# A graph and mixture-of-experts kernel on one NeuronCore: a fourth buffer for gathered rows, and inverse roots made on VectorE alone

## The reference

```python
x = x + gnn0(layernorm(x))   # h = n @ wl; sum over 100000 edges of w * h[src] into row dst; + n @ wr + biases
x = x + ffn0(layernorm(x))   # 8 experts on every node, mixed by gates
x = x + gnn1(layernorm(x))   # the same edges again, other weights
x = x + ffn1(layernorm(x))   # 32 experts, one chosen for each node

def ffn0(n):
    gate = softmax(n @ Wr + br)                       # [nodes, 8]
    h = relu(bn(n @ W1[e] + b1[e]))                   # for each expert e
    h = relu(bn(h @ W2[e] + b2[e]))
    return sum over e of gate[e] * (h @ Wo[e] + bo[e])

layernorm(x) = (x - mean) / sqrt(var + 1e-5)
bn(h) = g * (h - m) * rsqrt(v + 1e-3) + b
```

## Time and profile before

| | us |
|---|---|
| median of 3 runs | 2962.04 |
| lowest and highest | 2961.93, 2962.98 |
| the profiled execution, its own time | 2958.48 |
| its span (first to last instruction) | 2956.5 |

### The profile page before, as it was taken

How to read it: one execution, slowest core, us unless ns; L and a number is a source line. 1 busy time by engine, 2 the same in 40 slices (tenths; PEclk the granted TensorE clock), 3 DMA queues, 4 the chain that set the end, 5 groups by cost and what they waited for, 6 DMA issues and landing times. The chain is left out here.

```text
span 2956.5 us, 54481 instructions
## 1 busy us (share of the span) xinstructions
PE 2599.4 (88%) x19092; PEld 2420.7 (82%) x19092; DVE 2167.4 (73%) x5110; ACT 1565.7 (53%) x3295; POOL 1957.5 (66%) x1696
## 2 busy tenths in 40 slices
PE   5799935799999999999999994599999999999999
PEld 5799825788888888888888873489999999999999
DVE  8898836577787777777878754767777777777773
ACT  4477636788888888888888762111212112121212
POOL 0355557777777877777777501877777777777770
PEclk9999956799999999999999997689999999999999
DMA  2133454332333333233233203788888888888880
GB/s 74 6 82 77 93 137 144 91 97 78 109 108 91 99 108 110 79 107 110 78 115 108 80 1 114 212 205 214 204 215 214 212 208 215 213 213 209 212 212 24
DMA packets 241962, 390.31 MB, mean 132 GB/s; under 512 B 43642, under 2 KB 115218, under 8 KB 241426
## 3 DMA queue, kind: packets, MB, share of 16 engines
q0 software_dynamic: 163072, 310.24, 41.1%
q1 hardware_dynamic: 78324, 74.90, 8.0%
q10 hardware_dynamic: 288, 1.61, 0.1%
HBM read 343.43 MB, written 43.19 MB: 131 GB/s over the span
## 5 line engine op out<-in xcount | busy, mean ns | idle before, releaser
L1409 POOL DMA_INDIRECT f_got<-h_tab,list_cols x784 | 981.1, 1251 | 291.0 <-issue 219.1
L2121 POOL DMA_INDIRECT n_got<-h_tab,edge_cols x784 | 806.5, 1029 | 238.5 <-issue 227.6
L1690 DVE TENSOR_TENSOR f_hlo<-edge_cols,f_hhi 128x1024 fp32r<-128x1024 f32 (+1 forms) x208 | 242.0, 1163 | 294.3 <-ACT f_hhi L1498 294.1
L1585 PE MATMUL bank<-f_mhi,f_hot 128*128 128x256 f32 x1168 | 329.0, 311 | 131.2 <-DVE f_mlo L1684 131.1
L1468 ACT ACTIVATE f_got<-f_got,list_cols 128x256 f32<-128x256 f32 x784 | 333.9, 497 | 145.6 <-DMA f_got<-h_tab,list_cols 145.1
L2185 ACT ACTIVATE n_hrh<-bank 128x512 fp32r<-128x512 f32 x196 | 116.9, 597 | 535.6 <-PE bank L2254 535.6
L1585 PEld LDWEIGHTS bank<-f_mhi,f_hot 128*128 128x128 f32 x1168 | 247.6, 212 | 148.0 <-issue 143.8
L1493 ACT ACTIVATE edge_cols<-bank,f_shf,f_scl 128x512 f32<-128x512 f32 (+1 forms) x416 | 295.1, 743 | 106.9 <-PE bank L1400 76.7
L2232 PE MATMUL bank<-n_got,n_hot_h 128*128 128x256 f32 x784 | 242.2, 309 | 99.4 <-DMA n_got<-h_tab,edge_cols 59.0
L1586 PE MATMUL bank<-f_mlo,f_hot 128*128 128x256 f32 x1168 | 320.3, 304 | 0.0
L400 POOL DMA_INDIRECT list<-runs,off_i x98 | 158.0, 1612 | 215.2 <-DVE off_i L759 99.0
(11 more groups left out here) (331 smaller groups left out, 7833.0 us busy)
## 6 DMA issues: line engine op xcount, KB each, us to landing
f_got<-h_tab,list_cols POOLq DMA_INDIRECT x784
n_got<-h_tab,edge_cols POOLq DMA_INDIRECT x784, 3.8
n_rows<-acc_tab SPq DMA_DIRECT2D x24, 256.0 KB, 4.7
out_rows<-n_rows SPq DMA_DIRECT2D x24, 256.0 KB, 3.7
h_tab<-acc SPq DMA_DIRECT2D x37, 128.0 KB, 3.5
edge_cols<-in_w SPq DMA_DIRECT2D x16, 256.0 KB, 2.8
acc<-in_x SPq DMA_DIRECT2D x4, 896.0 KB, 7.9
h_tab<-hbuf SPq DMA_DIRECT2D x7, 512.0 KB
```

Of the source, the lines that this page charges most:

```text
L1409: nc.gpsimd.indirect_dma_start(got[:, s % RING0, u, :], None, h_tab[0], bass.IndirectOffsetOnAxis(gidx0[:, s * U + u:s * U + u + 1], 0), b ...
L1585: nc.tensor.matmul(tile_bank(t), lhs, mhi[:, s % 2, u, :], start=begins, stop=False)
L1690: nc.vector.tensor_tensor(hlo[l][:, :, 0:w], rl[:, :, 0:w], hhi[l][:, :, 0:w].bitcast(F32), ALU.subtract).then_inc(s_lo[l], 1)
L2121: nc.gpsimd.indirect_dma_start(got[:, s % RING, u, :], None, h_tab[1], bass.IndirectOffsetOnAxis(gidx[:, s * U + u:s * U + u + 1], 0), bou ...
```

## The change

Three edits, all in the second stage.

1. `RING0` is 4 instead of 3: four buffers for gathered rows, each for one slot (4 x 256 floats per partition). The tensor `x4` is gone; the third raw weight buffer now lies in the upper columns of `xraw`, which are not otherwise in use while weights load.
2. The square roots of both layer norms are no longer taken by ScalarE. VectorE computes the inverse root from `var` alone: it shifts the number's bits right by one, subtracts from a constant (the guess), and makes three Newton steps of three instructions each, 11 instructions (`ROOT_STEPS`) instead of 5. The waits for ScalarE (`s_sd`, `s_sd4`) are gone; VectorE waits for its own `s_var`, `s_var4`.
3. The root of batch norm is made by the same function, and its Sqrt on ScalarE is gone.

```diff
-RING0 = 3
+RING0 = 4
+SEED = float(0x5f3759df)
+ROOT_STEPS = 11
...
-            x4 = sb3("x4", [P, F, 2 * P])
...
-            raw = [rl[:, :, 0:D], rl[:, :, D:2 * D], x4[:, :, :]]
+            raw = [rl[:, :, 0:D], rl[:, :, D:2 * D], xraw[:, :, D:2 * D]]
...
-                    if s - 1 in READY:
-                        g = READY.index(s - 1)
-                        t, w = tile(g, 0), width(g)
-                        act.wait_ge(s_var, t + w)
-                        nc.scalar.activation(scale[:, t:t + w], var[:, t:t + w], ACT.Sqrt).then_inc(s_sd, 1)
...
-                    if s - 1 in DONE:
...
-                        nc.scalar.activation(scale[:, t:t + w], var[:, t:t + w], ACT.Sqrt).then_inc(s_sd4, 1)
...
-                        nc.scalar.activation(scl[:, :, :, :], bnt[:, :, :, :], ACT.Sqrt).then_inc(s_bnroot, 1)
...
+                def inverse_root(r, v, x, counter, base):
+
+                    bits, seed = v.bitcast(I32), r.bitcast(I32)
+                    nc.vector.tensor_scalar(x.bitcast(I32), bits, 1, None, ALU.arith_shift_right).then_inc(counter, 1)
+                    dve.wait_ge(counter, base + 1)
+                    nc.vector.tensor_scalar(seed, x.bitcast(I32), -1.0, SEED, ALU.mult, ALU.add).then_inc(counter, 1)
+                    for i in range(3):
+                        dve.wait_ge(counter, base + 3 * i + 2)
+                        nc.vector.tensor_tensor(x, r, r, ALU.mult).then_inc(counter, 1)
+                        dve.wait_ge(counter, base + 3 * i + 3)
+                        nc.vector.scalar_tensor_tensor(x, x, -0.5, v, ALU.mult, ALU.mult).then_inc(counter, 1)
+                        dve.wait_ge(counter, base + 3 * i + 4)
+                        nc.vector.scalar_tensor_tensor(r, x, 1.5, r, ALU.add, ALU.mult).then_inc(counter, 1)
+                    dve.wait_ge(counter, base + ROOT_STEPS)
...
                 def newton(t, w, counter, base):
-                    r, v, x = scale[:, t:t + w], var[:, t:t + w], nwt[:, t:t + w]
-                    nc.vector.reciprocal(r, r).then_inc(counter, 1)
...
-                    nc.vector.tensor_tensor(r, r, x, ALU.mult).then_inc(counter, 1)
-                    dve.wait_ge(counter, base + 5)
+                    inverse_root(scale[:, t:t + w], var[:, t:t + w], nwt[:, t:t + w], counter, base)
```

More of the change, by code:

```diff
@@ L1223, in build @@
             s_var = sem("f_var")
-            s_sd = sem("f_sd")
             s_newton = sem("f_newton")
@@ L1241, in build @@
             s_var4 = sem("f_var4")
-            s_sd4 = sem("f_sd4")
             s_newton4 = sem("f_newton4")
@@ L1483, in relus @@
                     if n == 0 and l == 0:
-                        act.wait_ge(s_bn, 10)
+                        act.wait_ge(s_bn, 5)
                         act.wait_ge(s_wlo, NPIECE)
@@ L1563, in _ @@
                             nc.scalar.activation(bos[at:at + EXPERTS0, :], braw, ACT.Copy).then_inc(s_bos, 1)
-                        act.wait_ge(s_bn, 1)
-                        nc.scalar.activation(scl[:, :, :, :], bnt[:, :, :, :], ACT.Sqrt).then_inc(s_bnroot, 1)
                     for i in range(s * PACE, min(s * PACE + PACE, NPIECE)):
@@ L1708, in add_out @@
                                                        ALU.mult, ALU.add).then_inc(s_out, 1)
-                def newton(t, w, counter, base):
-                    r, v, x = scale[:, t:t + w], var[:, t:t + w], nwt[:, t:t + w]
-                    nc.vector.reciprocal(r, r).then_inc(counter, 1)
[L1713 to L1719, removed]
-                    nc.vector.tensor_tensor(r, r, x, ALU.mult).then_inc(counter, 1)
-                    dve.wait_ge(counter, base + 5)
+                def inverse_root(r, v, x, counter, base):
[11 more added lines that the diff above has]
+                    dve.wait_ge(counter, base + ROOT_STEPS)
+                def newton(t, w, counter, base):
+                    inverse_root(scale[:, t:t + w], var[:, t:t + w], nwt[:, t:t + w], counter, base)
                 def logits(i):
@@ L1817, in _ @@
                         t, w = tile(g, 0), width(g)
-                        dve.wait_ge(s_sd, g + 1)
-                        newton(t, w, s_newton, 5 * g)
+                        dve.wait_ge(s_var, t + w)
+                        newton(t, w, s_newton, ROOT_STEPS * g)
                         if g:
@@ L1849, in _ @@
                         t, w = tile(g, 0), width(g)
-                        dve.wait_ge(s_sd4, g + 1)
-                        newton(t, w, s_newton4, 5 * g)
+                        dve.wait_ge(s_var4, g + 1)
+                        newton(t, w, s_newton4, ROOT_STEPS * g)
                         if g:
@@ L1873, in _ @@
                                                 bos[HI_A:HI_A + EXPERTS0, :].bitcast(F32), ALU.subtract).then_inc(s_bos, 1)
[L1874 to L1884, removed]
+                        dve.wait_ge(s_bn, 1)
+                        inverse_root(*(a[:, :, :, :].rearrange("p l e f -> p (l e f)") for a in (scl, bnt, shf)), s_bnroot, 0)
                         nc.vector.tensor_tensor(scl[:, :, :, :], scl[:, :, :, :], bnp[:, :, 1], ALU.mult).then_inc(s_bn, 1)
                         nc.vector.tensor_tensor(shf[:, :, :, :], bnp[:, :, 0], bnp[:, :, 3], ALU.subtract).then_inc(s_bn, 1)
-                        dve.wait_ge(s_bn, 8)
+                        dve.wait_ge(s_bn, 3)
                         nc.vector.tensor_tensor(shf[:, :, :, :], shf[:, :, :, :], scl[:, :, :, :], ALU.mult).then_inc(s_bn, 1)
-                        dve.wait_ge(s_bn, 9)
+                        dve.wait_ge(s_bn, 4)
                         nc.vector.tensor_tensor(shf[:, :, :, :], shf[:, :, :, :], bnp[:, :, 2], ALU.add).then_inc(s_bn, 1)
```

3 lines of the change are left out of this document (removed).

## The result

| | before | after |
|---|---|---|
| median, us | 2961.98 (4 runs) | 2933.11 (4 runs) |
| profiled execution, us | 2958.48 | 2933.08 |
| ratio to before, 95% interval | | 0.9893 (0.9876 to 0.991) |
| first gather of the second stage to first gather of the third, us | 1430.5 | 1404.5 |

The change makes the kernel 28.9 us faster by the medians and 25.4 by the profiled executions, where -33 was predicted. The last line of the table is 1837.3 - 406.8 against 1813.1 - 408.6: -26.0 us, all of the difference, in the second stage.

What follows compares the result with a forecast made beforehand. It took GpSimd's gathers to be as full as TensorE and their late edge stream to idle TensorE. -44 (ring) + 6 (gathers) + 0 (roots) + 4 (returning waits) + 1 (stage end) = -33 us: 2962 to 2929 us, range 2912 to 2952.

Steps and rivals of the forecast that it cites:

- GpSimd is as full as TensorE, and late gathers reach TensorE: Second stage, 609 to 1690 us: gathers fill 1017 of 1081 us; a 3.3 us GpSimd stall is paid back by TensorE.
- So every wait of the present pattern goes: Gathers waiting for a free buffer, 609 to 1690 us: four buffers allow 23.5 us for a 19.7 us lag, gain 44.
- my first rival: Second stage: the consumers are the limit, so the gain is 24 us, to 2938 us; chance 0.20.
- the second rival: Ring of gathers: a deeper ring only shifts the wait, leaving 44 us nearly whole, 2957 us; chance 0.06.
- Gathers lengthened by VectorE, +6: Gathers beside VectorE: same VectorE work in 3.5% less time, so a gather meets it 3.5% more often, +6 us.
- Roots 0 net: Layer norm roots: ScalarE's relief and VectorE's longer root taken as 0 us together, bounds -15 and +27.
- A root 2.54 us: Layer norm root on VectorE: nine two-input instructions at 0.20 and two `tensor_scalar`s at 0.37, 2.54 us instead of 1.18.
- The rival in which small `tensor_scalar`s wait out gathers: Roots on VectorE: two each wait for a whole gather, 26 us more, half on the path, 2942 us; chance 0.04.
- The end of the stage, +1: Last root, alone on the path to the second stage's end: 2.2 us instead of 1.29, +1 us.
- Slower, the longer roots pace VectorE: Rival: TensorE waits for `mlo` by all of each longer root, 27 us and 1, nothing from the ring, 2990 us; chance 0.05.
- The marks that I set: Profile after: `mlo` waits under 10 us, gathers 1.27 to 1.29, one Exp table load, group 102, last gather near 1640.

Runs made afterwards that it cites:

- e7: The changed kernel with `mlo` made ahead of the lower halves of the finished rows in slot 0 of a group: 2925.4 us, 0.986 of before.
- e8: As e7, and in one slot of each group `mlo` also made ahead of the output sums, only while there are edges: 2911.8 us, 0.981 of before.
- e9: The changed kernel with three buffers instead of four and one Newton step instead of three, roots still on VectorE: 2951.8 us, 0.995 of before.

## Why the prediction was right, and where its steps were not

**The time and its sign** were right: -28.9 us by the medians, -26.0 in the stage, for a forecast of -33, and inside the range. That the number came so near was in part luck, since large terms were wrong and made up for one another. As an account of GpSimd's time (where the time went, not what caused it):

| us | forecast | measured |
|---|---|---|
| waits for a full ring, all gathers (44.9 to 32.2) | -44 + 4 | -12.7 |
| length of the 784 gathers (981.1 to 959.2) | +6 | -21.9 |
| other pauses up to the last gather | 0 | -4.3 |
| from the last gather to the third stage | +1 | +13.0 |
| sum | -33 | -26 |

Of the steps:

- *GpSimd is as full as TensorE, and late gathers reach TensorE.* Right. The wait in front of `xhi` and its 2.36 us in place 11 were made by gathers: with four buffers ScalarE waits for no landing, and place 11 fell by 14 us.
- *"So every wait of the present pattern goes", gain 44.* **The step that failed.** Measured 44 to 32 net. I held the lag from gather to `mlo` fixed at 19.7 us. But it is not a property of the consumers: it grows as GpSimd runs ahead, and in the slots of places 0 and 1 it was 24 us on average after the change. Over slots 32 to 195 the lag was 21.5 us on average, where it had been 16.6. The ring gave what VectorE and ScalarE could take and filled again; that their order set the limit is what e7 and e8 show, which change nothing but that order and gain. This is the mechanism of my first rival, 2938 us with a chance of 0.20, whose time the result is as near to as to my own. What I counted against it, the 77 us of landings that ScalarE waited for, was real; the pace just stopped at the next limit. Of the second rival the waits came true (32 of 44 us stayed) and the time, 2957 us, did not: a ring that is full again once a group is no proof that nothing was gained.
- *Gathers lengthened by VectorE, +6.* Wrong in sign: the mean fell from 1.265 to 1.234 us, 650 x 0.031 = 20 us less. I scaled the meetings with density, as if they came at random. They don't: both engines run in a fixed pattern, and the pattern shifted. It was not that fewer gathers met one of the four large two-input subtractions and comparisons (`hot`, `mlo`, `hlo`, `xlo`): 290 began under one before and 299 after. Those that began under `hlo` (125 before, 129 after) took 1.54 us on average before and 1.37 after, which makes nearly all of the 20 us: they began later in it. What shifted the pattern is not shown.
- *Roots 0 net.* Right with four buffers, within a few us (-6.3 + 6.7 by the stage, -1.1 + 5.4 by the medians). With three buffers the two parts were -14 and +39; the second lies outside my bound of +27. What I did not see is that the fourth buffer is what makes the roots free.
- *A root 2.54 us.* Measured 2.19; the shift and the guess take 0.17 us each, my lower bound. The rival in which small `tensor_scalar`s wait out gathers is dead: these two, on int32, do not even show the 0.34 us of the float one.
- *The end of the stage, +1.* Right for the last root: 2.24 us from the end of `var` (1794.58) to the normalisation, for 1.29. Too small for the end as a whole, +13.0 from the last gather on. The gathers run further ahead, so the last `mlo` starts 19.1 us behind the last gather where it started 11.4 us behind (+7.7). Behind that `mlo` the stage took 153.7 us for 148.6 (149.0 with one Newton step). Three roots lie there, at 1676, 1727 and 1795 us, and I had counted one.
- *Slower, the longer roots pace VectorE.* Wrong for this change, but it is what three buffers do, and what six steps do with four.

The marks that I set: table loads and the last gather (1640) came as said, a group took 102.5 for 102. The mean length of a gather should have risen to 1.27 to 1.29 us and fell to 1.23. The waits for `mlo` should have fallen under 10 us and did not: at 32 us net they are nearer to the "some 40 us" that I had named as the sign of being wrong, and that was the mark of the failed step.

What I drew from the Trainium skill, "SBUF — State Buffer" ("Who interferes with whom"), was only half of it. The same section also says that a VectorE instruction with two inputs in SBUF contends with a GpSimd instruction that reads SBUF, and the traces agree with that if a gather is such an instruction: it is listed as reading `list_cols`. Of 75 gathers that began under the subtraction L1684 in the trace of before (600 to 1650 us) all took over 1.1 us, 1.84 on average. The blocking that it states for two-port modes did not show on gathers: the 39 that began under the normalisations L1826 and L1857 took 1.01.

## What to carry to other kernels

A full ring says that its consumers are late, and one buffer more shifts the meeting point. Waits for it are what is left over, not a price: in e9 they grew by 9 us while the kernel became 14 us faster. One buffer more gives at most what the consumers can take, so before counting the producer's waits as gain, ask what the consumers' own order would allow if data were always there. And price two edits together: the same longer chain cost 39 us with three buffers and 7 us with four (37 and 5 by the medians). Where several engines run fixed orders, find the longest unbroken run in front of the step that the bottleneck waits for. Two such moves, which add and remove no work, gave 32 us here by the stage and 26 by the medians, about as much as the change.

## What I had not expected of the hardware

- Whether a gather is lengthened depends on what VectorE runs as it begins. In the trace of before (600 to 1650 us) 194 gathers began ahead of one of the four large `tensor_tensor`s and had it start beside them: all took 1.0 us. Of the 287 that began under one, 267 ended 0.88 us after that instruction, 99 of them though another followed at once. It is not a strict rule: nine, also followed at once, ended only 0.88 us after the second (2.8 us long and more), and 11 were not lengthened. Under three `tensor_scalar`s in a row (1.20 us) a gather took its 1.01 us.
- A `tensor_scalar` of 128x4 takes 0.33 to 0.41 us on float32 beside gathers, 0.17 without them, and on int32 0.17 beside them too.
- In the change TensorE falls to 1.2 GHz eleven times between 700 and 1655 us. Ten of the falls come at the end of, or up to 1.5 us behind, the idle time of 2.3 us that each group has in place 15, one behind an idle time of 1.8 us. Such an idle time does not always bring one: in e7, with the same ten of 2.3 us, the clock falls six times. In e8, where TensorE is never idle for more than 0.87 us in this stretch, it never falls.
